# Two accumulating scatters in flight: a third row of the slot table says how many earlier ones a tile waits for

## The reference, cut to what matters

```python
x = x + tanh(g_xattn) * xattn(layernorm(x), ctx)
# the experts, on the new x:
xf = layernorm(xn)                        # 2048 x 256
topk_p, topk_i = top_k(probs, 2)
for eid in range(8):
    xe = xf * dense_gate[:, eid:eid + 1]
    gate, up = split(xe @ gate_up_w[eid].T)
    out = out + (silu(gate) * up) @ down_w[eid].T
x = x + tanh(g_ffn) * out
```

## Time and profile before

| | |
|---|---|
| time, median of 3 runs | 601.69 us (599.58 to 602.46) |
| profiled execution | 602.2 us (its span; the page gives no other time for it) |
| second part, from the first matmul of slot 1 to the end | 386.96 to 602.2 us |
| TensorE busy over the span | 522.3 us (87%) |
| GpSimd busy over the span | 231.9 us (39%) |
| scatters: instructions, mean time on GpSimd | 39, 1.585 us |

### The profile page before, as it was taken

How to read it: one execution, slowest core, us unless ns; L and a number is a source line. 1 busy time by engine, 2 the same in 40 slices (tenths; PEclk the granted TensorE clock), 3 DMA queues, 4 the chain that set the end, 5 groups by cost and what they waited for, 6 DMA issues and landing times.

```text
span 602.2 us, 12363 instructions
## 1 busy us (share of the span) xinstructions
PE 522.3 (87%) x3712; PEld 476.4 (79%) x3713; DVE 340.4 (57%) x783; ACT 282.2 (47%) x866; POOL 231.9 (39%) x319
## 2 busy tenths in 40 slices
PE   8999999999999999998998420699988998999991
PEld 6789999998989889898998410588877877888881
DVE  5856666677586585765756764255444544533330
ACT  3446556555465555564553112355543544533330
POOL 5160000337008780077704625043433433443333
PEclk9999999999999999999999755799999999999995
DMA  8500000001000100001010995636446436333322
GB/s 246 181 2 1 0 2 2 20 1 35 3 0 26 44 20 15 0 10 63 2 36 1 224 229 178 206 84 151 109 90 156 117 76 157 53 51 53 55 36 26
DMA packets 32372, 41.54 MB, mean 69 GB/s; under 512 B 3088, under 2 KB 28432, under 8 KB 32336
## 3 DMA queue, kind: packets, MB, share of 16 engines
q1 hardware_dynamic: 25184, 31.75, 17.9%
q0 software_dynamic: 7152, 9.33, 9.9%
HBM read 24.12 MB, written 16.95 MB: 68 GB/s over the span
## 4 chain that ended last, share of the span: by engine, by line
PE 34%; issue 26%; DVE 11%; ACT 8%; DMA 6%; POOL 6%; POOLq 3%; DVEq 2%; SPq 2%; another core or an unknown queue 1%; ACTq 0%
PE bank L603 7%; PE bank L581 6%; ACT probs L773 5%; PE bank L527 4%; POOL tok L1225 4%; PE bank L543 4%; PE bank L1279 3%; PE bank L557 3%; DMA expert_queue<-zrow 3%; DVE nmax L892 2%; POOLq L1233 2%; DMA out_dram<-yq,to_row 2%; PE bank L706 2%; PE bank L501 2%; DVEq L902 1%
## 5 line engine op out<-in xcount | busy, mean ns | idle before, releaser
L773 ACT ACTIVATE probs<-bank,nmax 128x154 f32<-128x154 f32 x256 | 97.6, 388 | 123.6 <-DVE nmax L892 119.3
L581 PE MATMUL bank<-vdiag,pT 128*128 128x128 f32 (+2 forms) x640 | 80.0, 272 | 7.1 <-DVE oT_lo L916 6.9
L581 PEld LDWEIGHTS bank<-vdiag,pT 128*128 128x128 f32 (+1 forms) x640 | 77.5, 191 | 10.5 <-DVE oT_lo L916 10.3
L1234 POOL DMA_INDIRECT out_dram<-yq,to_row x39 | 61.8, 1585 | 33.7 <-issue 24.1
L1279 PE MATMUL bank<-gu_hi,xqT_hi 128*128 x156 | 68.7, 441 | 1.1 <-DVE xqT_lo L1396 1.1
L892 DVE TENSOR_REDUCE nmax<-bank 128x2 f32<-128x308 f32 x128 | 60.1, 471 | 7.7 <-PE bank L543 6.8
L1279 PE MATMUL bank<-gu_hi,xqT_lo 128*128 x156 | 61.9, 397 | 0.0
L1279 PE MATMUL bank<-gu_lo,xqT_hi 128*128 x156 | 61.7, 396 | 0.0
L1408 DVE TENSOR_TENSOR hidT_lo<-bank,hidT_hi 128x512 fp32r<-128x512 f32 x39 | 26.9, 690 | 53.1 <-ACT hidT_hi L1355 53.1
L1403 DVE TENSOR_TENSOR hid<-hid,bank 128x512 f32<-128x512 f32 x39 | 26.8, 688 | 52.6 <-PE bank L1279 52.6
L557 PE MATMUL bank<-ident,probs 128*128 128x128 f32 (+1 forms) x320 | 46.2, 273 | 5.6 <-ACT xfT L786 2.9
(11 more groups left out here) (183 smaller groups left out, 1432.4 us busy)
## 6 DMA issues: line engine op xcount, KB each, us to landing
gu_raw<-in_gate_up_wT_dram SPq DMA_DIRECT2D x8, 1024.0 KB, 5.0
expert_queue<-zrow SPq DMA_DIRECT2D x8, 642.5 KB
xq<-expert_queue SPq DMA_DIRECT2D x39, 128.5 KB, 2.5
dn_raw<-in_down_wT_dram SPq DMA_DIRECT2D x8, 512.0 KB, 6.0
x<-in_x_dram SPq DMA_DIRECT2D x4, 512.0 KB, 13.0
out_dram<-out SPq DMA_DIRECT2D x8, 256.0 KB, 2.2
wq_raw<-in_L_xattn_Wq_dram SPq DMA_DIRECT2D x1, 1024.0 KB, 11.5
wo_raw<-in_L_xattn_Wo_dram SPq DMA_DIRECT2D x1, 1024.0 KB, 10.6
```

Of the source, the lines that this page charges most:

```text
L581: last = nc.tensor.matmul(at[:, col0 + j0 * DH:col0 + j0 * DH + n], pT[u % 2][0:rows, b, :], v, start=(b == 0), stop=(b == NBLK - 1), skip ...
L773: last = nc.scalar.activation(probs[u % 4][:, j * NKB:(j + 1) * NKB], S_BANK[hf][:, m * NKB:(m + 1) * NKB], ACT.Exp, bias=nmax[:, u % 4, j ...
L1234: nc.gpsimd.indirect_dma_start(out[:, :], bass.IndirectOffsetOnAxis(to_row[:, 0:1], 0), yq[p % 2][:, :], None, compute_op=ALU.add).then_in ...
```

## The change

The one semaphore `e_add` becomes two, one for scatters of even and one for scatters of odd slots, and `to_row` becomes two buffers. A scatter of tile j waits for all earlier scatters of its own parity, which means scatter j-2, and for a number of scatters of the other parity that is read from a third row of `table` into a register: all of them when the tile is the first of its expert or empty, all but the latest one otherwise. The value is at least one scatter (16), so slots 1 and 2 wait for all earlier ones as well. `scaled` waits for the scatter j-2 as before, now by the semaphore of its parity. The table's third row is made by five more instructions on VectorE after the table's second row, from the starts of the experts, which are therefore kept (`start_row` takes the place of the overwritten `start`), and from one more iota on GpSimd early in the kernel.

```diff
+            start_row = asb("start_row", [P, E]); opens = asb("opens", [P, MT]); half_no = asb("half_no", [P, MT + 1])
...
+                nc.gpsimd.iota(half_no[:, :], [[1, (MT + 1) // 2], [0, 2]], base=-1, channel_multiplier=0, allow_small_or_imprecise_dtypes=True)
...
+                then(v.tensor_tensor(past[:, :, :], slots, start[:, :].unsqueeze(1).to_broadcast(by_slot), ALU.is_equal))
+                then(v.tensor_reduce(opens[:, :], past[:, :, :], AX_X, ALU.add))
+                then(v.scalar_tensor_tensor(opens[:, :], none_left[:, :], 1.0, opens[:, :], ALU.min, ALU.add))
+                then(v.tensor_tensor(opens[:, :], opens[:, :], half_no[:, 1:MT + 1], ALU.add))
+                then(v.tensor_scalar(table[:, 2, :], opens[:, :], 1.0, 16.0, ALU.max, ALU.mult)).then_inc(s["waves"], 1)
...
             def scatter_add(i, p):
                 j = RT * i + p
+                if not (isinstance(j, int) and j == 0):
+                    others = pool.value_load(table[0:1, 2, bass.ds(j, 1)] if not isinstance(j, int) else table[0:1, 2, j:j + 1],
+                                             min_val=16, max_val=16 * (MT // 2 + 1))
                 pool.wait_ge(s["e_ysb"], j + 1)
                 pool.wait_ge(s["e_tok"], j + 1)
-                at_least(pool, s["e_add"], 16 * j)
-                nc.gpsimd.tensor_tensor(to_row[:, :], tok[p][:, :], no_offset[:, :], ALU.add).then_inc(s["e_idx"], 1)
+
+                at_least(pool, s["e_add"][p % 2], 16 * ((RT // 2) * i + p // 2))
+
+                if not (isinstance(j, int) and j == 0):
+                    pool.wait_ge(s["e_add"][1 - p % 2], others)
+                nc.gpsimd.tensor_tensor(to_row[p % 2][:, :], tok[p][:, :], no_offset[:, :], ALU.add).then_inc(s["e_idx"], 1)
                 nc.gpsimd.drain()
-                nc.gpsimd.indirect_dma_start(out[:, :], bass.IndirectOffsetOnAxis(to_row[:, 0:1], 0), yq[p % 2][:, :], None,
-                                             compute_op=ALU.add).then_inc(s["e_add"], 16)
+                nc.gpsimd.indirect_dma_start(out[:, :], bass.IndirectOffsetOnAxis(to_row[p % 2][:, 0:1], 0), yq[p % 2][:, :], None,
+                                             compute_op=ALU.add).then_inc(s["e_add"][p % 2], 16)
...
             tokens(0, 1)
+            pool.wait_ge(s["waves"], 1)
...
-            pool.wait_ge(s["e_add"], 16 * MT)
+            for n in range(2):
+                pool.wait_ge(s["e_add"][n], 16 * ((MT + 1 - n) // 2))
...
                 act.wait_ge(s["e_y"], j + 1)
-                at_least(act, s["e_add"], 16 * (j - 1))
+                at_least(act, s["e_add"][p % 2], 16 * ((RT // 2) * i + p // 2))
```

More of the change, by code:

```diff
@@ L107, in gated_xattn_moe @@
                      "xstat xrstd xn xres "
-                     "w_in w_hi w_lo eT_ps eT_hi eT_lo e_gate e_silu e_up e_hid e_hT_ps e_hT_hi e_hT_lo e_y e_ysb e_tok e_idx e_add").split():
+                     "w_in w_hi w_lo eT_ps eT_hi eT_lo e_gate e_silu e_up e_hid e_hT_ps e_hT_hi e_hT_lo e_y e_ysb e_tok e_idx waves").split():
             s[name] = sem("s_" + name)
         for name, n in dict(x_in=4, wk_in=2, scores=2, smax=2, exp=2, o_sb=2, ot_ps=2, ot_hi=2, ot_sb=2, proj=5, proj_hi=5, proj_sb=5,
-                            stat1=2, stat2=2, var=4, rstd=4, xin=2, xfT_sb=2, xq_in=2).items():
+                            stat1=2, stat2=2, var=4, rstd=4, xin=2, xfT_sb=2, xq_in=2, e_add=2).items():
             s[name] = [sem(f"s_{name}{k}") for k in range(n)]
@@ L118, in gated_xattn_moe @@
         tgx = sb("tgx", [P, 1]); tgf = sb("tgf", [P, 1])
-        table = sb("table", [P, 2, MT], U16)
+        table = sb("table", [P, 3, MT], U16)
         order = sb("order", [P, E], U16)
@@ L136, in gated_xattn_moe @@
             tok = [fsb(f"tok{n}", [P, 1], U32) for n in range(RT)]
-            to_row = fsb("to_row", [P, 1], U32); no_offset = fsb("no_offset", [P, 1], U32)
+            to_row = [fsb(f"to_row{n}", [P, 1], U32) for n in range(2)]; no_offset = fsb("no_offset", [P, 1], U32)
             xqT_hi = fsb("xqT_hi", [P, KD, P], F32R)
@@ L1178, in _ @@
                 then(v.tensor_tensor(within[:, :, :], within[:, :, :], past[:, :, :], ALU.subtract))
-                then(v.scalar_tensor_tensor(start[:, :], expert_no[:, :], -float(REG // P), start[:, :], ALU.mult, ALU.add))
-                then(v.tensor_tensor(past[:, :, :], slots, start[:, :].unsqueeze(1).to_broadcast(by_slot), ALU.subtract))
+                then(v.scalar_tensor_tensor(start_row[:, :], expert_no[:, :], -float(REG // P), start[:, :], ALU.mult, ALU.add))
+                then(v.tensor_tensor(past[:, :, :], slots, start_row[:, :].unsqueeze(1).to_broadcast(by_slot), ALU.subtract))
                 then(v.tensor_tensor(past[:, :, :], past[:, :, :], within[:, :, :], ALU.mult))
```

## The result

| | before | after |
|---|---|---|
| time, median of 4 runs | 601.14 us (599.58 to 602.46) | 592.84 us (591.40 to 595.04) |
| ratio, 95% interval | | 0.9865 [0.9823, 0.9908] |
| profiled execution, span | 602.2 us | 589.6 us |
| slot 5 opens (TensorE) | 406.98 | 403.53 |
| slot 5 to slot 38 | 174.03 us | 167.19 us |

The opening of slot 5 differs by 3.45 us between the two profiled executions, and lies anywhere from 403.5 to 410.8 in the executions shown here.

What follows compares the result with a forecast made beforehand. GpSimd's chain of scatters, 5.36 us each, was taken to bound the slots; 12.9 us of TensorE's stalls and 5.1 of end backlog off 602.2 gave 584.2, a median of 583.7 us with the offset; range 581.0 to 589.5.

Steps and rivals of the forecast that it cites:

- What bounds the kernel: Over the 39 slots: GpSimd's scatters run one after the other, 5.36 us each, and hold TensorE.
- TensorE's own rate: Slots 5 to 10: TensorE needs 4.88 us a slot when nothing else reaches it.
- one scatter more in flight: Scatter j waits for j-2; GpSimd's own 2.84 us a period is below 4.88, so TensorE bounds the slots.
- Loads and `yq`: With GpSimd on time, token copies end 3.4 us into the slot before the tile's own; queue-row waits go.
- The sum: Slot 38 opens at 568.1, 12.9 us gained; the end comes at 584.2, 18.0 us gained in all.
- The register load: GpSimd, each slot but the first: some 0.6 us with register work, costing nothing below 2.0 us a slot.
- the rival that ended slower: GpSimd's register load can't finish while a scatter is in flight, adding 0.6 us in 38 slots: 624 us; chance 0.05.
- The tiles that wait for all: Slots 7, 13, 19, 23, 27, 31, 34 and empty 37, 38 keep the old chain: 5.07 us a link.
- The table's third row and the iota: Five more VectorE instructions, at most 2.4 us, and 0.18 us on GpSimd, both in idle time: no cost.
- The first: Rival: weight loads go on holding TensorE; 595.7 us, 590 with half of it; range 587 to 596, chance 0.14.
- The second rival: GpSimd's register load waits for the scatter in flight, so scatters stay one after the other: 624 us, chance 0.05.
- the offset: Profiled execution taken as 0.5 us above the median, turning 584.2 us into a median of 583.7.

Runs made afterwards that it cites:

- the version without drains: Changed kernel with GpSimd's drain between copy and scatter replaced by a semaphore wait, carried by a 128x1 add: 588.57 us, ratio 0.9754.
- the run in which all tiles wait: Changed kernel with the table's third row saying all in every slot; two semaphores, two buffers and register load stay: 606.67 us, ratio 1.0066.
- the run with the second drain: Kernel before the change, with another drain added right behind the scatter instruction: 624.18 us in a single run.

## Why the prediction was wrong

**What bounds the kernel** was right, and so was TensorE's own rate: 4.88 us was forecast, and the version without drains runs all 33 slots at 4.85 with TensorE busy in all of it.

**The step that failed** is in "one scatter more in flight": "What GpSimd does itself in a period, from the copy into `to_row` to the end of the token copy, is 579.69 - 576.85 = 2.84 us". 1.06 of it was the way from the copy to the scatter, taken as work. It holds a drain, and the drain was read where nothing was in flight: in the kernel before, each one stood right behind the wait for the landing, and took 0.37 us (median). In the changed kernel, where most have a scatter in flight, it takes 3.0 (median), and copy to scatter becomes some 3.4 us (533.51 to 536.87). The change removed the wait by which the drain was cheap. The row that could have warned is the pair "copy, 0.86 us of issue, scatter" of the earlier trace rows: idle time ended by "issue" is a cost that the semaphores don't explain, and I moved it into another state without asking what it does there.

**Loads and `yq`** failed with it. I had the token copy end 3.4 us into the slot before the tile's own. In the slow slots the drain ran up to 5.0 us, the token copy behind it came late, and TensorE waited 2.3 us in all for queue rows. `yq`, which was to wait for no scatter, waited 20.4 us. That "the waits for queue rows go" came true in the version without drains, and there `yq` waits for no scatter.

**The sum**: 12.9 us up to slot 38 measured 6.84, and slot 38 to the end, forecast as 16.1 (584.2 - 568.1), measured 18.88. What failed at the end is one term: scatter 36, forecast 1.65 us into slot 38, went out 4.93 us into it (575.65 - 570.72), behind a drain that waited for scatter 35; what follows it took 13.95 us, 14.4 by the forecast. Without drains 14.07 us are gained up to slot 38, and from there to the end it takes 18.24, with scatter 36 going out 1.36 us into the slot. The forecast's 16.1 is not reached there either, since the last drain takes 3.25 us, a cost that the forecast didn't know.

**The register load** was bounded rightly: 0.276 us on GpSimd's sequencer. Even in the chain of the run in which all tiles wait, two semaphores and the load together cost 2.6 us from slot 5 to the end at most, far below the 22 of the rival that ended slower. It is not what is missing.

**The tiles that wait for all**: 585.48 - 580.54 = 4.94 us a link at the end, 5.07 forecast. **The table's third row and the iota**: no cost, as forecast. VectorE idles 1.71 us for ScalarE's split behind the five new instructions, 4.36 before without them.

**The rivals.** The first has its time (590 to 595.7) near the measured one, and even its sign, TensorE waiting for queue rows in four slow slots beside or after weight loads. It is not the cause: the version without drains loads the same weights at the same places, and its TensorE isn't held once. Landings beside weights are slow there too: a scatter that goes out at 431.85, during a weight load, has its last packets at about 436.8, 4.9 us later; in the changed kernel one of 427.42 has them at about 432.9, 5.5 later. In the changed kernel the drain of the next scatter waits for that landing, and the next scatter goes out 6.64 us behind; in the version without drains it goes out 4.81 us behind. The second rival had the right kind of mechanism, an instruction on GpSimd that can't pass a scatter in flight, at the wrong instruction.

**Median and span**: the changed kernel's profiled execution took 591.40 us around a span of 589.6. So 1.8 us lie outside the span, and by the same 1.8 the execution of before with its span of 602.2 took some 604.0 us, more than any of its timed runs (602.46 at the most). The 0.5 us that I took for the offset was not one of span to time.

## What to carry to other kernels

Before a wait is relaxed so that two DMAs of one engine overlap, look what else on that engine waits for them: here a drain between two GpSimd instructions waited for the engine's indirect DMA in flight, and it read cheap only where a semaphore had waited first. Where the drain is only there to order a copy before its reader, the copy's own semaphore can do that; here that alone was worth as much as the whole change with its drain (0.9865 each), and the two together gave 0.975. The price of an instruction is read in the state that the change will leave, not in the one it removes.

## What the runs showed of the hardware

- A drain on GpSimd with an accumulating scatter in flight takes 3.0 us (median of the changed kernel), and 4.1 when it stands right behind the scatter, whose instruction is over after 1.56; with none in flight 0.29 to 0.37 (medians). In the run with the second drain it lasts up to 8.1 us where the landing takes up to 7.8.
- Scatters that were not drained left a cost to the next drain: 3.25 us at the end of a kernel after 39 of them, 0.125 where each slot drains; 5.9 us for one put in slot 38, beside a landing.
- A scatter's packets began 2.1 us after its instruction's start, also 2.3 us behind another scatter; beside a weight load they began 3.8 and 4.4 us after it (431.85 and 427.42 in the paragraph on the rivals).
- Adding an unused tile of 4 bytes a partition changed TensorE's free slot from 4.88 to 4.85 us, with nothing else edited (one execution; the other versions with the tile show 4.85 too).
